# Order of GpSimd, VectorE and ScalarE steps in the attention of a fused two-layer kernel

## The reference

```python
xn = _layernorm(x, axis=-1)
x = x + _L1_attn_ref(xn, ...) + _L1_ffn_ref(xn, ...)

# attention: 16 heads of 8, over the first axis, 8 long, for each of the 512 positions
attn = jnp.einsum('nqd,nkd->nqk', q, k) * scale
attn = jax.nn.softmax(attn, axis=-1)
out = jnp.einsum('nqk,nkd->nqd', attn, v)
out = out @ out_w.T + out_b

# feed-forward: 16 experts of width 64, the best four weighted by `combine`, and a shared one
g = jax.nn.silu(jnp.einsum('th,efh->tef', x, w1_e))
u = jnp.einsum('th,efh->tef', x, w3_e)
routed = jnp.einsum('tef,ehf,te->th', g * u, w2_e, combine)
```

## Time and profile before

| | us |
|---|---|
| median of three timed runs | 355.44 (355.14 to 356.28) |
| profiled execution | 355.92 |
| its span in the trace | 354.1 |
| stage of the 72 slices in the trace, about | 164 to 351 |

### The profile page before, as it was taken

One profiled execution on the slowest core, in us unless ns is written; L12 is line 12 of the kernel. 1 busy time (PEld: TensorE's weight loads), 2 busy tenths in 40 slices (PEclk: granted clock), 3 DMA queues, 4 the chain that ended last, 5 costly groups with the idle time before them and its releaser, 6 DMA issues.

```text
span 354.1 us, 5666 instructions
## 1 busy us (share of the span) xinstructions
PE 304.5 (86%) x1771; PEld 252.0 (71%) x1771; DVE 311.0 (88%) x826; ACT 178.9 (51%) x499; POOL 250.2 (71%) x162
## 2 busy tenths in 40 slices
PE   0568877899898987589999999899998999989995
PEld 0246555777686776477877887698987888878785
DVE  4995899979879677976999999899998999989795
ACT  3345766778786767677242531613516235162520
POOL 4184667826557361117999899989999899988671
PEclk9996999999999999879999999999999999999999
DMA  5590000000000000004853332423424334253102
GB/s 142 161 302 9 2 0 1 2 1 1 3 0 3 0 0 3 0 4 122 182 128 93 102 105 90 118 61 91 149 82 111 120 94 115 59 148 114 38 2 59
DMA packets 21321, 24.91 MB, mean 70 GB/s; under 512 B 2420, under 2 KB 12060, under 8 KB 21292
## 3 DMA queue, kind: packets, MB, share of 16 engines
q1 hardware_dynamic: 20248, 24.09, 24.7%
q10 hardware_dynamic: 820, 0.39, 0.4%
q0 software_dynamic: 224, 0.08, 0.1%
HBM read 22.19 MB, written 2.36 MB: 69 GB/s over the span
## 4 chain that ended last, share of the span: by engine, by line
DVE 37%; PE 34%; POOL 12%; issue 10%; ACT 6%; DMA 1%; DVEq 0%; POOLq 0%; ACTq 0%
PE Q L944 16%; PE VN L944 8%; PE T L944 7%; POOL prod_qk L874 6%; POOL prod_pv L884 4%; DVE hid L1632 4%; DVE rope_b L1368 3%; DVE rope_a L1366 3%; DVE att L1591 2%; PE T L940 2%; DVE sgc L1619 2%; DVE scr L1577 2%; DVE bst L1209 2%; DVE attn L1398 2%; DVE xT_lo L1419 1%
## 5 line engine op out<-in xcount | busy, mean ns | idle before, releaser
L874 POOL TENSOR_TENSOR prod_qk<-qkv 128x1024 f32<-128x1024 f32 x32 | 76.6, 2412 | 2.9 <-DVE above L1461 2.1
L884 POOL TENSOR_TENSOR prod_pv<-prob,qkv 128x1024 f32<-128x1024 f32 x32 | 69.0, 2195 | 7.4 <-DVE att L1591 5.1
L773 ACT ACTIVATE Q<-Q 128x512 f32<-128x512 f32 x48 | 27.5, 581 | 56.5 <-PE Q L944 56.3
L1632 DVE TENSOR_TENSOR hid<-T,sgc 128x512 f32<-128x512 f32 x64 | 43.4, 679 | 0.1
L944 PE MATMUL Q<-bias,ones 128*128 128x400 f32 (+1 forms) x64 | 30.3, 474 | 15.2 <-ACT v_ext L663 7.1
L1577 DVE TENSOR_REDUCE scr<-prod_qk 128x128 f32<-128x1024 f32 x32 | 38.8, 1211 | 5.0 <-POOL prod_qk L874 5.0
L944 PEld LDWEIGHTS Q<-w,hid 128*128 128x128 f32 x288 | 37.5, 191 | 3.4 <-DVE hid L1632 0.6
L944 PEld LDWEIGHTS VN<-w,hid 128*128 128x128 f32 x288 | 37.6, 191 | 3.1
L944 PE MATMUL Q<-w,hid 128*128 128x128 f32 x288 | 38.0, 275 | 0.4 <-DVE hid L1632 0.4
L944 PE MATMUL T<-xT_hi,w_hi 128*128 128x512 f32 x72 | 31.2, 434 | 8.2 <-DVE hid L1632 7.9
L1591 DVE TENSOR_REDUCE att<-prod_pv 128x128 f32<-128x1024 f32 x32 | 38.2, 1195 | 0.0
(11 more groups left out here) (186 smaller groups left out, 801.1 us busy)
## 6 DMA issues: line engine op xcount, KB each, us to landing
cw<-comb_table SPq DMA_DIRECT2D x62, 256.0 KB, 4.6
out_x<-fin SPq DMA_DIRECT2D x7, 256.0 KB, 4.5
x<-in_x SPq DMA_DIRECT2D x2, 256.0 KB, 3.1
wraw<-in_w1T SPq DMA_DIRECT2D x1, 512.0 KB, 4.2
w3raw<-in_w3T SPq DMA_DIRECT2D x1, 512.0 KB, 4.9
w<-in_w2T SPq DMA_DIRECT2D x1, 512.0 KB, 5.9
cw<-comb_table SPq DMA_DIRECT2D x4, 128.0 KB, 3.1
rope_s<-in_c_sin ACTq DMA_DIRECT2D x1, 256.0 KB, 5.1
```

The costliest lines, as they stand in the source:

```text
L773: act.activation(gated[:, :], gate_bank(n, s)[:, :], ACT.Silu).then_inc(sg_ready, 1)
L874: pool.tensor_tensor(prod_qk[:, t % 2], bc(qkv2[:, TH * half + t, j, 0:D], 1, NB), qkv2[:, :, j, D:2 * D], ALU.mult).then_inc(qk_prod, 1)
L884: pool.tensor_tensor(prod_pv[:, t % 2].rearrange("p (h e) b -> p b h e", e=HD), bc(prob[:, t].rearrange("p h b -> p b h"), 3, HD), qkv2[:, ...
L1632: V.tensor_tensor(hid[:, s % 3, :], UB[k][:, :], src, ALU.mult)\
```

## The change

On POOL, the third score product of the next unit is issued between the third and the fourth value product. The bias is added by unit (four batches of one tile of positions) and no longer by batch, and later: in units 3 to 6 that of the unit before, in unit 7 two, ahead of and behind `normalise`. On DVE, the sum of the probabilities goes from p = 5 to p = 3, ahead of the first value sum, and its reciprocal from p = 6 to p = 4, behind the second value sum; in unit 7 they go from p = 2 and 3 to the same places. The score sums of units 3 and 5, which begin eight slices behind the unit before, come one slice later; those of the other units stay. On ACT, the exponential of unit 7 goes from p = 1 to p = 2.

```diff
                 for u, p in units(k):
-                    if p == (1 if u == END else 2):
+                    if p == 2:
                         exp_done(u)
...
-            def biased(c):
-                if c == 0:
+            def biased(n):
+                j, half = place(n)
+                b = slice(TH * half, TH * half + TH)
+                if n == 0:
                     pool.wait_ge(ld_w2, 64)
-                pool.wait_ge(xn2_ready, 2 * c + 2)
-                pool.tensor_tensor(x[:, c], x[:, c], bc(bout2[:, :], 1, NJ), ALU.add).then_inc(x_biased, 1)
+                    pool.wait_ge(xn2_ready, 2 * TH)
+                if n == TH:
+                    pool.wait_ge(xn2_ready, 2 * NB)
+                pool.tensor_tensor(x[:, b, j, :], x[:, b, j, :], bc(bout2[:, :], 1, TH), ALU.add)\
+                    .then_inc(x_biased, 1)
...
-            def products_pv(n, j):
+            def products_pv(n, j, which):

                 pool.wait_ge(p_ready, n + 1)
-                for t in range(TH):
+                for t in which:
...
                 next_qk(0)
-                if n + 2 < NB:
-                    biased(n + 2)
+                if 3 <= n < END:
+                    biased(n - 1)
                 less_max(n)
                 next_qk(1)
-                products_pv(n, n % NJ)
+                products_pv(n, n % NJ, range(3))
                 next_qk(2)
+                products_pv(n, n % NJ, range(3, TH))
                 next_qk(3)
+                if n == END:
+                    biased(END - 1)
                 normalise(n)
+                if n == END:
+                    biased(END)
...
-                dve.wait_ge(x_biased, TH * half + TH)
+                dve.wait_ge(x_biased, n + 1)
...
-                first = (-4, -3, -2, -1) if u == 0 else (-7, -6, -1, 0) if u == END else (-8, -7, -2, -1)
+                short = u > 0 and BASE[u] - BASE[u - 1] < NS
+                first = (-4, -3, -2, -1) if u == 0 else (-7, -6, -1, 0) if short else (-8, -7, -2, -1)
                 if p in first:
                     scores(u, first.index(p))
                 if p == 0:
                     row_max(u)
-                if p == (2 if u == END else 5):
+                if p == 3:
                     sum_of_p(u)
-                if p == (3 if u == END else 6):
-                    over_sum(u)
                 if 3 <= p < 3 + TH:
                     values(u, p - 3)
+                if p == 4:
+                    over_sum(u)
```

## The result

The changed kernel takes 360.28 us against 355.38 of the kernel before, a ratio of 1.0143 (95% interval 1.0127 to 1.0159): 4.9 us slower, where +4.3 and 359.7 had been forecast. Its profiled execution took 360.02, with a span of 358.2.

A forecast was written before the change was run, and what follows sets the result against it. DVE was taken as the bound, PE standing behind it, so its gaps decide. 4.1 - 2.2 + 0.8 - 0.7 + 2.5 = +4.5, taken as +4.3: from 355.44 to 359.7 us, range 358.3 to 361.0, chance 0.70.

The forecast's parts named there:

- waits at the fourth value sum: DVE, units 0 to 6: the fourth value sum newly waits for POOL's value product, 0.1 to 0.9 each, +4.1 us.
- second score sums of units 3 and 5: DVE: sums one slice later shrink the gap of 1.21 to 0.06 and close that of 1.08, -2.2 us.
- bias ahead of `less_max`, units 4 and 6: POOL: bias holds `less_max` 0.78 late, so second score sums show gaps of 0.84 for 0.22 and 0.69, +0.8 us.
- Silu wait in slice 34 and small gaps: DVE's gap of 0.59 behind unit 3's exponential closes, with a few tenths of PE gaps, -0.7 us.
- last exponential: ACT, unit 7: exponential behind unit 6's copy, so DVE waits 4.4 for slice 67's Silu in place of 1.9, +2.5 us.
- A: Rival: the hole at the end does not open, the exponential starting with `less_max`; +0.6, 356.0 us; chance 0.12.
- C: Rival: no hole at the end and no wait at the fourth value sum; -3.5, 351.9 us; chance 0.05.
- B: Rival: fourth value sum does not wait, POOL's third value product at least 0.8 earlier; +0.2, 355.6 us; chance 0.09.
- D: Rival: value products at the longer pace everywhere and a bias without cover, 0.6 + 1.3 more, 361.6 us; chance 0.04.

The follow-up runs named there:

- e7: Kernel before, with only the last exponential moved to p = 2 (unit 7's probability sum and reciprocal at p = 3 and 4): 357.64 us.
- e3: Changed kernel with the third score product behind the fourth value product again: 356.09 us.
- e1: Changed kernel with the copy `attT_evac` of unit 6 one slice later, behind the Silu of slice 67: 356.72 us.
- e5: Changed kernel with the score sums of units 3 and 5 back one slice earlier: 363.18 us.
- e4: Changed kernel with the probability sum and its reciprocal back at p = 5 and 6 in units 0 to 6: 358.63 us.
- e9: Changed kernel: third score product and probability sums (units 0-6) back, e1's copy move, bias out of units 3-5, unit 7's second score sum a slice later: 349.03 us.

## Why the prediction was right, step by step

| step | forecast | measured in the changed kernel |
|---|---|---|
| waits at the fourth value sum | +4.1, seven of 0.1 to 0.9 | 3.9 in six rows, 0.32 to 0.97; 0.09 in unit 1, too short for a note in a row |
| second score sums of units 3 and 5 | -2.2 | 1.08 gone, 1.21 down to 0.02 |
| bias ahead of `less_max`, units 4 and 6 | +0.8 | 0.76 and 0.68 for 0.22 and 0.69: +0.5 |
| Silu wait in slice 34 and small gaps | -0.7 | 0.59 gone, and 0.13 at a Silu in unit 5 |
| last exponential | +2.5 | row maximum of unit 7 to last `fin` 22.04 for 19.54: +2.5; 2.52 by e7 |
| sum | +4.3 | +3.9 in idle times of DVE, +4.55 in the stage, +4.9 in the time |

The idle times grow by 0.6 less than the stage. The forecast counted distances between starts, and a row counts idle time from the end of the instruction before, which is 0.08 later than the next one would have started; for the seven waits at the fourth value sum that makes 0.6, an estimate. It fits e3, which has none of them: the stage without DVE's idle times is 166.0 us before, 166.7 in the changed kernel and 166.0 in e3.

**Right.** The subtraction of starts (what DVE does between first and fourth value sum, against what POOL does) gave each of the seven waits within 0.2 us. The last exponential was right in place and size. PE's transposes stood behind an up product that waited 0.50 for `hid` of slice 64 and began at 334.23; the loop order over u puts the copy first, and the load comes behind the copy; e1, with the copy taken away, has the load right behind the Silu and the exponential right behind `less_max`. What the Trainium skill says (ScalarE: Activation LUTs, Step-by-step: what each stage is for), that the load is placed right before the activation that needs it, agrees with the rows at 337.17 and, in e1, at 331.17, which stand next to their exponentials on ACT.

**Mis-sized.** The bias: I had `less_max` 0.78 late, so gaps of 0.84. In unit 5 it is 290.16 against 289.49 (the row maximum at 288.74 and the 0.75 behind it), so 0.67, and the gap is 0.68. The score sums: e5 puts their worth at 2.6 in the stage where my sum has -2.2 + 0.8 - 0.7 = -2.1. By its rows, 2.28 of waits come back at the score sums of units 3 and 5, 0.68 of the price in units 4 and 6 goes, and 0.87 comes at two Silus, where my 0.7 had one; that is 2.5 of the 2.6.

**Right sum, reason in part wrong.** For unit 4 I took POOL's wait for the first value sum to grow beyond the 0.83 of the earlier trace rows; it fell to 0.06. I left out what my own next step says: the wait of 1.21 at the second score sum, ahead of that first value sum, is gone, so the value sum stands at 274.75 and not 1.21 later, and POOL hardly waits for it. The chain over the first value sum that I added up is there, and the wait is 0.65 where I had 0.8; but POOL's own queue is only 0.13 shorter than that chain, so unit 4 is of the kind that I saw in units 3 and 5 alone, and that its number came out is in part luck. e4 tells the two kinds apart: it closes 0.32 to 0.64 where POOL waits for the first value sum, and leaves two thirds of the waits where it hardly does.

**Rivals.** A (no hole at the end) and C with it fall by the wait of 4.2, B by the six `att` rows, D by POOL's value products (2.19 us on average, 2.20 before) and by the bias in unit 6, behind which POOL still waits 0.37 for the row maximum.

## What to carry to other kernels

Where three engines are nearly full, count an order by the gaps of the engine that all others wait for: for each data handover, what that engine has queued between the two ends, against what the other one has. Filling another engine's wait with work is no gain if the work then stands between that engine and the next handover. And an instruction moved past a slice boundary is moved past everything that shares the slice: look up what the loop issues ahead of it, and what that waits for.

## What was not expected

PE. In the nine-slice units its matmuls are busy nearly all the time, so I expected 1 to 2 us of e9's gain to come back there. Nothing did: in a unit where DVE has no gap PE is busy 21.55 of 21.79 us, and DVE waits for it nowhere but at the last `fin`. The waits of its weight loads for `hid` fell from 19.5 us to 13.0 in e9. So those busy shares held slack. The Trainium skill (Perfetto Trace Analysis, Identifying the Most-Contended Engine) says that the matmuls' busy share is not a good measure of how close PE is to its roofline, since pipelined instructions look smaller in a trace than they are. That the share is a poor measure, these runs bear out: 21.55 of 21.79 us, and DVE not held up. The page's reason they do not show.

The time ahead of the stage. The row maximum of unit 0 starts between 174.73 (e4) and 176.89 (e9) in these ten profiles. TensorE's granted clock, where 1.00 stands for 2.4 GHz and a lower mean for a stretch partly at 1.2 GHz, is 1.00 in the first 90 us of e4 and 0.96 in the other nine, and 0.97 to 0.99 in the 60 us behind them in all ten. From 150 to 174 us it is 0.85 in e9 and 0.90 to 0.96 in the others. That is 2.2 us which no part of the change touches, as much as most of the single effects; how much of it is the clock's, these profiles do not separate. In e3 the clock fell in the tail, 0.90 from 330 us on against 0.98 in the changed kernel. It fell after two pauses of PE in the hole of 4.2 us (0.70 and 1.35); the changed kernel has the same hole and kept its clock there. Eight down products at 340.35 then took 1.91 us, against 1.05 at 345.09; PE shows no wait from there to the last output product, and DVE's wait for that one is 2.23 against 1.62. A comparison of stages inside the traces, taken beside the times, leaves out what lies ahead of the stage, but not such a fall inside it.
